# A graph network of four layers: all values ahead of the feed-forward products, second queries and keys between the first scores

## The reference

```
layer 0  h = (eps * h + adj @ h) @ W1 + b1            # 1024 wide
         out = silu(rmsnorm(h) * w) @ W2 + b2
layer 1  att = sigmoid(s1_i + s2_j + b) * adj * masks, rows divided by their sum
         out = att @ (h @ W + b)
layer 2  scores = q @ k.T / sqrt(32) + adj * w_e[head], -inf where adj is 0   # 8 heads
         out = softmax(scores) @ v @ Wo
layer 3  out = D^-1/2 adj D^-1/2 @ (h @ W3) + b3      # D: row sums of adj
```

## Time and profile before

| what | value |
|---|---|
| median of 3 runs | 3564.24 us (3564.21 to 3565.22) |
| the profiled execution | 3567.06 us, span 3565.2 us |
| PE busy in the span | 3447.6 us (97%) |
| DVE busy | 2655.7 us (74%) |
| ACT busy | 2286.7 us (64%) |
| POOL busy | 943.1 us (26%) |
| mean granted clock of TensorE | 0.994 |

### The profile page before, as it was taken

One profiled execution on the slowest core, in us unless ns is written; L12 is line 12 of the kernel. 1 busy time (PEld: TensorE's weight loads), 2 busy tenths in 40 slices (PEclk: granted clock), 3 DMA queues, 4 the chain that ended last, 5 costly groups with the idle time before them and its releaser, 6 DMA issues.

```text
span 3565.2 us, 70163 instructions
## 1 busy us (share of the span) xinstructions
PE 3447.6 (97%) x19886; PEld 2560.3 (72%) x20108; DVE 2655.7 (74%) x6794; ACT 2286.7 (64%) x5062; POOL 943.1 (26%) x2379
## 2 busy tenths in 40 slices
PE   6999999999999999999999999999999999999997
PEld 4777777777777777777777777777777777777774
DVE  6777777777787777777777877777777778777774
ACT  4666666666676666666666776666766667766664
POOL 2222331222322223322223212233222232122320
PEclk8999999999999999999999999999999999999999
DMA  3233223232232332232322223322323222323212
GB/s 102 50 94 90 76 65 88 59 95 74 73 83 64 84 94 71 65 95 53 95 77 74 79 71 77 95 71 71 89 53 95 81 75 75 76 72 95 71 54 65
DMA packets 166941, 275.09 MB, mean 77 GB/s; under 512 B 23908, under 2 KB 59876, under 8 KB 166760
## 3 DMA queue, kind: packets, MB, share of 16 engines
q1 hardware_dynamic: 164200, 269.25, 28.3%
q10 hardware_dynamic: 2560, 4.20, 0.6%
HBM read 122.37 MB, written 16.78 MB: 39 GB/s over the span
## 4 chain that ended last, share of the span: by engine, by line
PE 76%; issue 8%; ACT 7%; DVE 4%; DMA 3%; SPq 2%; DVEq 0%; POOL 0%; ACTq 0%; POOLq 0%
PE turn L1361 10%; PE value L1376 7%; PE score L1403 6%; PE front L1256 6%; PE front L1192 6%; PE score L1352 6%; PE front L1162 5%; PE front L1164 5%; PE front L1163 5%; ACT prob L646 3%; PE score L1349 3%; PE front L1219 2%; DMA qk_stack<-qk 2%; ACT pT L655 2%; PE score L1393 2%
## 5 line engine op out<-in xcount | busy, mean ns | idle before, releaser
L646 ACT ACTIVATE prob<-prob,small 128x512 f32<-128x512 f32 x1024 | 737.5, 720 | 351.7 <-DVE small L1001 344.3
L1001 DVE CUSTOM_DVE_ANT_0 prob<-score,adj_sb,drv 128x512 f32<-128x512 f32 x1024 | 759.2, 746 | 192.7 <-PE score L1352 184.7
L1361 PE MATMUL turn<-ident,prob 128*128 128x128 f32 x4096 | 626.1, 275 | 50.7 <-ACT prob L646 45.1
L1352 PE MATMUL score<-qk_stack 128*128 128x512 f32 x1024 | 592.2, 582 | 21.8 <-DMA qk_stack<-qk 21.7
L1361 PEld LDWEIGHTS turn<-ident,prob 128*128 128x128 f32 x4096 | 479.7, 141 | 181.4 <-issue 64.8
L655 ACT ACTIVATE pT<-turn 128x512 f32<-128x512 f32 x768 | 449.0, 585 | 72.5 <-PE turn L1361 42.3
L449 POOL TENSOR_TENSOR small<-small 128x1 f32<-128x1 f32 x128 | 24.9, 195 | 1401.2 <-ACT aside L580 1401.2
L758 DVE TENSOR_TENSOR s_lo<-front,s_hi 128x512 fp32r<-128x512 f32 x316 | 216.7, 686 | 151.5 <-ACT s_hi L539 151.5
L1349 PE MATMUL score<-unlinked,neg_mask 128*128 128x512 bf16 x802 | 306.1, 382 | 0.3 <-DVE small L1001 0.3
L1162 PE MATMUL front<-w_hi,s_hi 128*128 128x256 f32 x1024 | 300.6, 294 | 0.8 <-DVE w_lo L758 0.8
L1163 PE MATMUL front<-w_lo,s_hi 128*128 128x256 f32 x1024 | 288.3, 282 | 0.0
(11 more groups left out here) (209 smaller groups left out, 7871.6 us busy)
## 6 DMA issues: line engine op xcount, KB each, us to landing
qk_stack<-qk SPq DMA_DIRECT2D x992, 128.0 KB, 2.4
adjT_f<-in_adjT SPq DMA_DIRECT2D x32, 1024.0 KB, 5.2
adj_sb<-in_adj SPq DMA_DIRECT2D x32, 1024.0 KB, 7.5
prob<-in_adjT SPq DMA_DIRECT2D x32, 1024.0 KB, 5.3
x_new<-in_x SPq DMA_DIRECT2D x32, 512.0 KB, 4.2
out<-x_out SPq DMA_DIRECT2D x32, 512.0 KB, 3.0
qk_stack<-qk ACTq DMA_DIRECT2D x32, 128.0 KB, 2.6
pT<-in_W SPq DMA_DIRECT2D x2, 1024.0 KB, 10.9
```

Of the source, the lines that this page charges most:

```text
L646: act.activation(prob[:, i % 8, :], prob[:, i % 8, :], ACT.Exp, bias=nmax[:, h, n:n + 1], scale=-1.0, accum_out=prsum[:, h, n:n + 1]).then ...
L1001: dve.tensor_tensor_reduce(out=prob[:, i % 8, :], in0=SB_[i % 2][:, :], in1=adj_sb[:, n, :], scale=neg_w[:, h:h + 1], scalar=3e38, op0=ALU ...
L1352: pe.matmul(SB_[i % 2][:, :], qk_stack[:, h % 4, 0, tile(n)], qk_stack[:, h % 4, 1, :], start=False, stop=True).then_inc(sc_ps, 1)
L1361: last = pe.transpose(TB[k % 2][:, tile(n)], prob[:, (4 * h + n) % 8, tile(j)], ident[:, :])
```

## The change

- PE makes both halves of the values right behind the first queries and keys, ahead of `hidden(tf, 0, 0)`. The second half goes into `TB[0]` and not into `VB`. ACT copies both ahead of the first squares. The first head's transposes wait for that copy.
- The second queries are projected in step -3, behind score 1, and the keys in step -1, behind score 3 (before: step 0, ahead of score 4, and step 2, behind score 6). Their high parts are at steps 3 and 4 (before 2 and 4), both low parts at step 5 ahead of DVE's copy (before: step 3, and step 5 behind the copy).
- Tile 0 of the feed-forward network takes the steps of the others: scaling at step -1 (before -3), tanh and silu at 0 and 1 (tanh -2 and 0, silu -1 and 0), its transposes on PE behind those of steps 1 and 2 (before 0 and 1), high and low parts at 2 and 3 (before 1 and 2).
- The degrees move from steps 4, 6, 12 and 13 to 13, 14, 21 and 22, and `degrees` on POOL behind `hidden_norm` of tile 3.

```diff
@@ -220,9 +220,8 @@
             return (u - 11,) if 11 <= u < 15 else ()
         GRID = range(-4, 4 * H)
-        QK1_STEP, QK1_HIGH, QK1_LOW = (0, 2), (2, 4), (3, 5)
-        DEG_STEPS = (4, 6, 12, 13)
-        TANH_STEPS, SILU_STEPS, LOW_STEPS = (2, 4), (3, 4), (5, 6)
+        QK1_STEP, QK1_HIGH, QK1_LOW = (-3, -1), (3, 4), 5
+        DEG_STEPS = (13, 14, 21, 22)
         def hidden_bank(tf, n, c):
@@ -235,6 +234,10 @@
         def qk_bank(g, i):
             return (FB[2], VB)[i] if g else SB_[i]
+
+        def v_bank(j):
+
+            return TB[0] if j else VB
         def linear_bank(n):
@@ -496,11 +499,13 @@
                     hidden_norm(tf, 0)
                     hidden_norm(tf, 1)
                 if t is not None:
-                    degrees(t)
                     widen_inverse(t, 0)
                 if tf is not None:
                     hidden_norm(tf, 2)
                     hidden_norm(tf, 3)
+                if t is not None:
+                    degrees(t)
+                if tf is not None:
                     layernorm_tile(tf, 0, 1, f_norm, norm_tiles(0))
                     layernorm_tile(tf, 1, 1, f_norm, norm_tiles(0))
                 if t is not None:
@@ -638,7 +643,7 @@
             def values(t, j):
                 act.wait_ge(v_ps, at(t, 2, j + 1))
-                act.activation(vals[:, 2 * j:2 * j + 2, :].rearrange("p a d -> p (a d)"), VB[:, :], ACT.Copy).then_inc(v_ready, 1)
+                act.activation(vals[:, 2 * j:2 * j + 2, :].rearrange("p a d -> p (a d)"), v_bank(j)[:, :], ACT.Copy).then_inc(v_ready, 1)
             def exps(t, i):
                 h, n = divmod(i, NT)
@@ -674,11 +679,11 @@
                     qk_high(t, 0, 0)
                     qk_high(t, 0, 1)
                     stack_high(t)
+                    values(t, 0)
+                    values(t, 1)
                 if f:
                     square(tf, 0, 0)
                     square(tf, 0, 1)
-                if b:
-                    values(t, 0)
                 for g in GRID:
                     if g in prepare:
                         prepare[g]()
@@ -686,16 +691,10 @@
                         for n, u in tile_steps(g):
                             if n and u in (1, 2):
                                 square(tf, n, u - 1)
-                            elif n == 0 and u in TANH_STEPS:
-                                tanh(tf, n, TANH_STEPS.index(u))
-                            elif n == 0 and u in LOW_STEPS:
-                                hidden_hi(tf, n, LOW_STEPS.index(u))
-                            elif n and u in (4, 5):
+                            elif u in (4, 5):
                                 tanh(tf, n, u - 4)
-                            elif n and u in (6, 7):
+                            elif u in (6, 7):
                                 hidden_hi(tf, n, u - 6)
-                    if b and g == -2:
-                        values(t, 1)
                     if b and g in QK1_HIGH:
                         qk_high(t, 1, QK1_HIGH.index(g))
                     if b and g + 4 < 4 * H:
@@ -1061,15 +1060,11 @@
                         bias(t, g + 4)
                     if f:
                         for n, u in tile_steps(g):
-                            if u == (3 if n else 1):
+                            if u == 3:
                                 hidden(tf, n)
-                            elif n == 0 and u in SILU_STEPS:
-                                silu(tf, n, SILU_STEPS.index(u))
-                            elif n == 0 and u in LOW_STEPS:
-                                hidden_lo(tf, n, LOW_STEPS.index(u))
-                            elif n and u in (4, 5):
+                            elif u in (4, 5):
                                 silu(tf, n, u - 4)
-                            elif n and u in (6, 7):
+                            elif u in (6, 7):
                                 hidden_lo(tf, n, u - 6)
                     if b and g == 4 * H - 5:
                         inverse(t, 1)
@@ -1084,13 +1079,14 @@
                         prepare[g]()
                     if b and g in DEG_STEPS:
                         degree(t, DEG_STEPS.index(g))
+                    if b and g == QK1_LOW:
+                        qk_low(t, 1, 0)
+                        qk_low(t, 1, 1)
                     if b and g >= 0 and g % 4 == DVE_TURN:
                         turned_probs(t, g // 4)
                     if f and g == 4 * H - 4:
                         logits1(tf, (0,))
                         logits2(tf, (0,))
-                    if b and g in QK1_LOW:
-                        qk_low(t, 1, QK1_LOW.index(g))
                     if b and g == 4 * HG - 2:
                         inverse(t, 0)
                     if b and g == 4 * HG + 4:
@@ -1309,7 +1305,7 @@
                 if g == 1:
                     if i == 1:
-                        pe.wait_ge(v_ready, at(t, 2, 2))
+                        pe.wait_ge(v_ready, at(t, 2, 1))
                     elif later(t):
                         pe.wait_ge(out_ready, at(t, 4, 0))
                 elif i == 0:
@@ -1324,19 +1320,16 @@
                                    (bT_hi[:, k, :], bT_lo[:, k, :]), k == 0, k == DT - 1)
                 last.then_inc(qk_ps, 1)
-            def project_v(t, j, parts=(0, 1)):
-                if j and 0 in parts:
-                    pe.wait_ge(v_ready, at(t, 2, 1))
-                elif not j and later(t):
+            def project_v(t, j):
+                if not j and later(t):
                     pe.wait_ge(o_ready, at(t, 3, 0))
-                for i in parts:
+                for i in range(2):
                     for k in range(DT):
                         s = tile(2 * j + i)
-                        last = product(VB[:, D * i:D * i + D], (bT_hi[:, k, s], bT_lo[:, k, s]),
+                        last = product(v_bank(j)[:, D * i:D * i + D], (bT_hi[:, k, s], bT_lo[:, k, s]),
                                        (wp_hi[:, WV, k, :], wp_lo[:, WV, k, :]), k == 0, k == DT - 1)
-                if 1 in parts:
-                    last.then_inc(v_ps, 1)
+                last.then_inc(v_ps, 1)
             def scores(t, i):
                 h, n = divmod(i, NT)
@@ -1357,6 +1350,8 @@
                     pe.wait_ge(exped, at(t, 32, 4 * h + 4))
                 k = turn_of_prob[h, j]
                 wait_bank(t, k)
+                if h == 0 and v_bank(1) is TB[k % 2]:
+                    pe.wait_ge(v_ready, at(t, 2, 2))
                 for n in range(NT):
                     last = pe.transpose(TB[k % 2][:, tile(n)], prob[:, (4 * h + n) % 8, tile(j)], ident[:, :])
                 last.then_inc(b_turned, 1)
@@ -1428,22 +1423,19 @@
                 if b:
                     project_qk(t, 0, 0)
                     project_qk(t, 0, 1)
+                if b:
+                    project_v(t, 0)
+                    project_v(t, 1)
                 if f:
                     hidden(tf, 0, 0)
                     hidden(tf, 0, 1)
-                if b:
-                    project_v(t, 0)
                 if shared is not None:
                     shared()
                 for g in GRID:
                     if shared is not None and g == 6:
                         pe.wait_ge(setup_dve, SETUP_W2)
-                    if b and g == QK1_STEP[0]:
-                        project_qk(t, 1, 0)
                     if b and 0 <= g < 4 * H - 4:
                         scores(t, g + 4)
-                    if b and g == QK1_STEP[1]:
-                        project_qk(t, 1, 1)
                     if b and g in (4 * HG + 1, 4 * HG + 3):
                         attend(t, 0, g - 4 * HG - 1)
                         attend(t, 0, g - 4 * HG)
@@ -1455,14 +1447,14 @@
                                 turn_hidden(tf, n, u - 5)
                             for q in quarters(n, u):
                                 down(tf, n, q)
-                    if b and g in (-2, -1):
-                        project_v(t, 1, (g + 2,))
                     if b and g < 0:
                         scores(t, g + 4)
+                    if b and g in QK1_STEP:
+                        project_qk(t, 1, QK1_STEP.index(g))
                     if b and g >= 0:
                         turn_probs(t, g // 4, g % 4)
-                    if b and f and g in (0, 1):
-                        turn_hidden(tf, 0, g)
+                    if b and f and g in (1, 2):
+                        turn_hidden(tf, 0, g - 1)
                     if b and g == 4 * HG + 3:
                         turn_inverse(t, 0)
                 if b:
```

## The result

The changed kernel takes 3606.88 us (median of 4, 3604.61 to 3608.53) against 3564.73 of the kernel before: a ratio of 1.0116, with a 95% interval of 1.0099 to 1.0134. That is 42.1 us more. The forecast was 3601, in a range of 3563 to 3613.

What follows compares the result with a forecast made beforehand. A pass was taken as TensorE's in-order work plus its waits on the bias-to-exponential chain. Terms of 0.45, 0.40 and 0.36 gave 1.21 us a pass, 37.5 us in 31, on 3564.24: 3601 us, range 3563 to 3613.

Steps and rivals of the forecast that it cites:

- opening, up to the third head's transposes: From the start of a pass to the third head's transposes: TensorE comes 0.45 us a pass late.
- degrees at 13 and 14: A degree between DVE's copy of step 13 and the reciprocal delays tile 2's scaling and silu: 0.40 us a pass.
- degrees at 21 and 22: The degree at step 22 delays bias 27 and tile 3's scaling, up to exponential 31: 0.36 us a pass.
- Values ahead: Start of the pass: the DMA wait is covered, but the whole chain of biases begins 0.81 us later.
- Dense steps of tile 0: Feed-forward tile 0, between exponentials 3 and 7: exponential 7 starts at 1212.17, the second head's transposes 1.12 us late.
- Low parts and the early degrees: DVE, step 5 to bias 11: less work behind the copy cuts the lateness from 1.12 to 0.45 us.
- Small things: Other moves, wait counts and the last pass's half-clock start: put at nothing; second values there worth 0 to 1.7 us, once.
- Rival (a): Late degrees are hidden and only the opening's 0.45 us a pass stays: 3578 us; chance 0.20.
- Rival (b): The opening's DMA wait and third-head wait vanish, about 1.2 us a pass faster: 3526 us; chance 0.13.
- Rival (c): The opening comes out even at the third head's transposes and late degrees are hidden: 3564 us; chance 0.08.
- (d): Exponential 7 comes later still, the opening alone costs 0.9, in all 1.9 us a pass: 3623 us; chance 0.07.

Runs made afterwards that it cites:

- degrees_in_waits: Changed kernel with three degrees at step 15 ahead of tile 2's scaling, where DVE waits for GpSimd, and one at step 21: 3581.12 us.
- degrees_13_14: Changed kernel with the degrees of steps 13 and 14 kept and the other two at step 15, where DVE waits: 3594.8 us.
- degrees_21_22: Changed kernel with the degrees of steps 21 and 22 kept and the other two at step 15, where DVE waits: 3593.2 us.
- values_only: Kernel before with only the values moved: both halves ahead of the feed-forward products, their copies ahead of ACT's squares: 3593.18 us.
- keys_later: Changed kernel with the second keys projected at step 2 again: 3605.03 us.
- old_tile0_steps: Changed kernel with feed-forward tile 0 back on its old, spread steps: 3585.8 us.
- low_ahead_only: Kernel before with one line moved: the second low part of step 5 ahead of DVE's copy, not behind it: 3547.35 us.
- both_in_waits: Kernel before with step 5's low part ahead of DVE's copy and the degrees in DVE's waits (three at step 15, one at 21): 3544.56 us.

## Why the prediction was right, and by how much each term

| term | forecast, us a pass | in the trace | by an experiment |
|---|---|---|---|
| opening, up to the third head's transposes | 0.45 | 0.52 | 0.44 (degrees_in_waits over before) |
| degrees at 13 and 14 | 0.40 | 0.31 up to step 17 | 0.44 (degrees_13_14 over degrees_in_waits) |
| degrees at 21 and 22 | 0.36 | 0.42 from step 17 to 28 | 0.40 (degrees_21_22 over degrees_in_waits) |
| sum | 1.21 | 1.25; 1.23 over all passes | 0.44 + 0.44 + 0.40 = 1.28 |

Over the first 30 passes the experiments give 0.50 + 0.43 + 0.37 = 1.30, and the changed kernel is 1.30 longer: the three terms are the whole of it. That the sum was met to 0.02 is closer than its terms, which are off by up to 0.07 either way. (1.21 in 31 passes on 3564.24 is 3601.7, so the figure 3601 should have been 3602.)

- *Values ahead.* The first score no longer waits for the DMA, and the first bias is 0.84 late (1214.56 - 14.32 = 1200.24 against 1199.40), for 0.81 forecast. That this costs and doesn't gain is shown by values_only.
- *First head's transposes.* 0.49 late for 0.41, with a wait of 0.26 for 0.2 to 0.4.
- *Dense steps of tile 0.* Exponential 7 started 8.03 us after exponential 3; tile 1's 7.51 and one high part had given 8.19. The second head's transposes were 1.13 late for 1.12. This closeness is luck: exponential 3 came 0.08 later than forecast (1218.38 - 14.32 = 1204.06), the chain was 0.16 shorter, and the transposes followed exponential 7 by 0.95 and not 0.86. keys_later shows that PE's work there doesn't matter, old_tile0_steps that the steps do.
- *Low parts and the early degrees.* They took back 0.61 of that, for 0.67. low_ahead_only and both_in_waits give the shares, on the kernel before: the low part 0.62 of 0.69, the degrees 0.07.
- *Late degrees.* Both terms right, and additive. The trace's 0.31 is read at tile 2's transposes on PE; those of the probabilities right behind them are 0.88 late (1252.88 - 14.32 against 1237.68), which makes the two terms 0.36 and 0.37. One reading was wrong: the forecast has the copy of step 13 wait for PE at 1230.02, but in the kernel before it stands right behind the degree of that step (1229.38, 0.68 long) with no idle time. It waits for PE only in the changed kernel, 0.55 us. The step of the argument that carried both terms holds: not how much stands on the engine, but behind which wait and ahead of which.
- *The mis-sized term.* "Small things" stood at nothing, with 0 to 1.7 us to gain in the last pass. It went the other way, because the forecast took the stretch at half clock to begin with the work, and it begins before it (last section). The work at half clock (windows view: start and end, length, then busy us by engine, granted clock, DMA share, GB/s) now fills 6.40 us, 3.40 in the earlier trace rows:

```profile
3519.70:3526.10 6.40, 6.34 (x15) 4.15 (x16) 2.44 (x7) 1.87 (x5) 0.00 (x0) 0.51 0.92 205
```

The values did not keep the clock up. 3 us more of work at half clock are, by my estimate from these two stretches, 1.5 us lost, against up to 1.7 gained in the forecast; the last pass as a whole was 2.6 longer, and the cause of the rest stays open. Its length isn't steady from kernel to kernel (87.8 in keys_later, which differs only in where the second keys are projected; 84.9 in values_only), and the executions of the changed kernel differ by 3.9 us. So of the 5 us between 37 forecast and 42 measured 1 is the pass, 1.23 for 1.21, and 3 are the ends, which these runs don't resolve.

Rival (a), hidden late degrees, fell with degrees_13_14 and degrees_21_22. Rival (b), waits of the opening that simply go, fell with values_only and by its own sign: exponential 7 had to start by 1211.2 and started at 1226.41 - 14.32 = 1212.09. Rival (c), no change, and (d), 1.9 a pass, are excluded by the time.

## What to carry to other kernels

In a pipeline of engines that take their instructions in order, find for each engine the instruction that waits, and the next one that another engine waits for. Work between these two is paid, however idle the engine is, less the slack of what follows (0.43 and 0.37 of 0.60 us for the two late degrees that count); the same work just ahead of the waiting instruction is free up to the length of the wait. Two orders of the same instructions differed by 77 us here (3607 and 3530). And if the same chain already runs in another place of the kernel under other cover, its start-to-start time there prices the new place (8.19 us forecast, 8.03 measured): compare it with the work of the bound engine under it.

## What was not expected of the hardware

More work of the last pass ran at half clock in the changed kernel, though half clock lasted no longer. The last pass on PE, before and then changed (timelines of PE):

```profile
3480.79 0.79 PE L1352 MATMUL score<-qk_stack 128*128 128x512 f32 x1 [5.09 <-DMA qk_stack<-qk]
```

```profile
3517.41 0.39 PE L1342 MATMUL score<-unlinked,neg_mask 128*128 128x512 bf16 x1 [1.45 <-DVE unlinked L971]
3519.76 0.79 PE L1345 MATMUL score<-qk_stack 128*128 128x512 f32 x1 [1.96 <-DMA qk_stack<-qk]
```

The idle times look different but are much alike. The single 5.09 is a gap in the records: the weight load of the edge-mask matmul stands at 3478.43 in that trace too, 2.93 us after the load ahead of it and 2.25 ahead of the next, and only the matmul itself is missing. In the changed kernel the same two gaps between weight loads are 1.64 and 2.25.

Now the stretches ahead of these in the earlier trace rows and of the one shown above, before and then changed; the third column from the right is the granted clock:

```profile
3475.30:3481.00 5.70, 0.61 (x5) 0.51 (x4) 2.48 (x3) 1.64 (x3) 0.00 (x0) 0.71 0.56 120
```

```profile
3514.45:3519.70 5.25, 1.91 (x15) 1.42 (x13) 2.48 (x3) 1.97 (x4) 0.00 (x0) 0.95 0.56 119
```

A mean of 0.71 over 5.70 us is 3.3 us at the lower level of 1.2 GHz (0.50); with the 3.40 of the earlier trace rows that is 6.7 us. A mean of 0.95 over 5.25 us is 0.5, and 0.51 over 6.40 us is 6.3: 6.8 us. Before, the clock was down from 3.1 us ahead of the first score's product on (0.50 from 3477.7 to 3480.8), so that nearly half of the stretch passed in the wait for the DMA; in the changed kernel it fell 0.5 us ahead of it, and nearly all of the stretch met work. The earlier trace rows alone doesn't show this, as it begins where the work begins. Over the whole of the time behind the last edge mask the granted clock is almost the same, 0.92 and 0.91.

That an idle TensorE falls to half clock is what the Trainium skill says ("TensorE: Matmul & The Clock Gate", What's actually happening), and the trace agrees. When it falls was not to be had from the rows of the kernel before, and no run here shows what sets it: in keys_later, after idle times of 1.94 and 1.92 us at the same place, only about 3.4 us were at half clock. In the steady pass shown of each kernel, where the profile has no wait of PE above 0.60 us, the granted clock is 1.00.
